# Mixer: the four z products of a block moved into the slot of ScalarE's silu pass, and silu of z read from PSUM

## The reference

```python
def mamba2_mixer(xn, in_proj_w, conv_w, conv_b, dt_bias, A_log, D_skip, rms_w, out_proj_w):
    zxbcdt = xn @ in_proj_w
    z = zxbcdt[..., :D_INNER]
    xBC = zxbcdt[..., D_INNER:D_INNER + CONV_DIM]
    dt = zxbcdt[..., D_INNER + CONV_DIM:]
    dt = jax.nn.softplus(dt + dt_bias)
    xBC = jax.nn.silu(causal_conv1d(xBC, conv_w, conv_b))
...
    y = ssd_scan(xh, dt, Bm, Cm, A)
    y = y + D_skip[None, None, :, None] * xh
    y = y.reshape(*y.shape[:-2], D_INNER)
    y = y * jax.nn.silu(z)
    y = y * jax.lax.rsqrt(jnp.mean(jnp.square(y), axis=-1, keepdims=True) + 1e-05) * rms_w
    return y @ out_proj_w
```

## Time and profile before

| | us |
|---|---|
| median of 3 runs | 3185.32 (3183.98 to 3193.42) |
| the profiled execution, its own time | 3180.88 |
| its span | 3179.2 |
| PE busy | 2799.2 (88%) |
| DVE busy | 1839.9 (58%) |
| ACT busy | 1384.6 (44%) |
| POOL busy | 678.1 (21%) |

### The profile page before, as it was taken

The page is one execution under the profiler, slowest core; times in us unless marked ns, Lnnn a source line. Parts: engine busy times, 40 slices in busy tenths (PEclk is TensorE's granted clock), DMA queues, the critical chain, the costliest instruction groups (busy, mean ns, idle before and its releaser), DMA issues. The chain is left out here.

```text
span 3179.2 us, 46142 instructions
## 1 busy us (share of the span) xinstructions
PE 2799.2 (88%) x16998; PEld 2086.3 (66%) x16998; DVE 1839.9 (58%) x3504; ACT 1384.6 (44%) x2394; POOL 678.1 (21%) x716
## 2 busy tenths in 40 slices
PE   0488888888888888869999799999999999999999
PEld 0354555455555555458888687887878787878787
DVE  4688888888888888746767433333333333333332
ACT  0566666666666666536555322222222222222221
POOL 5022222222222222210000122222222222222221
PEclk6799989998999899879999899999999999999999
DMA  3010101010101010035211100000000000000000
GB/s 125 29 35 20 35 20 35 20 35 20 35 21 35 21 35 11 28 104 208 70 62 64 48 13 7 11 14 16 14 16 14 16 14 16 14 16 14 16 14 8
DMA packets 104858, 107.06 MB, mean 34 GB/s; under 512 B 35897, under 2 KB 98617, under 8 KB 102977
## 3 DMA queue, kind: packets, MB, share of 16 engines
q1 hardware_dynamic: 99520, 103.81, 10.1%
q10 hardware_dynamic: 5120, 0.19, 0.1%
HBM read 71.41 MB, written 40.94 MB: 35 GB/s over the span
## 5 line engine op out<-in xcount | busy, mean ns | idle before, releaser
L1597 PE MATMUL fbank<-hid,fw 128*128 128x512 f32 x4096 | 962.3, 395 | 0.0
L1597 PEld LDWEIGHTS fbank<-hid,fw 128*128 128x128 f32 x4096 | 766.1, 187 | 187.0
L1747 DVE TENSOR_TENSOR hid<-fhf,hid 128x512 fp32r<-128x512 f32 x384 | 264.9, 690 | 704.3 <-POOL hid L1704 704.3
L1704 POOL TENSOR_SCALAR hid<-fhf 128x512 fp32r<-128x512 f32 x384 | 271.1, 706 | 1040.2 <-ACT fhf L1676 760.8
L808 ACT ACTIVATE mh<-ebank 128x512 f32<-128x512 f32 x512 | 302.0, 598 | 415.0 <-PE ebank L663 413.8
L1121 DVE SCALAR_TENSOR_TENSOR mh<-mh,gm 128x512 f32<-128x512 f32 x512 | 403.2, 794 | 1.8 <-ACT mh L808 1.8
L663 PE MATMUL ebank<-cright,cleft 102*128 102x512 bf16 x512 | 211.1, 413 | 64.1 <-ACT cin L847 28.9
L1676 ACT ACTIVATE fhf<-fbank,sh2c 128x512 f32<-128x512 f32 x128 | 88.0, 688 | 382.4 <-PE fbank L1597 382.4
L676 PE MATMUL yin<-mh,xpad 128*32 128x128 f32 x4096 | 230.5, 300 | 27.1 <-DVE mh L1121 26.6
L650 PE MATMUL ebank<-ah,win 128*128 128x512 f32 x640 | 246.7, 425 | 7.1 <-ACT cin L847 6.6
L1676 ACT ACTIVATE fhf<-fbank,sh1c 128x512 f32<-128x512 f32 x128 | 88.1, 688 | 320.8 <-PE fbank L1597 320.6
(11 more groups left out here) (180 smaller groups left out, 4380.1 us busy)
## 6 DMA issues: line engine op xcount, KB each, us to landing
fx<-x_d SPq DMA_DIRECT2D x17, 512.0 KB, 3.9
xs<-in_x SPq DMA_DIRECT2D x16, 512.0 KB, 4.3
h_d<-in_h SPq DMA_DIRECT2D x16, 512.0 KB, 5.4
o_d<-o SPq DMA_DIRECT2D x16, 512.0 KB, 2.9
mo<-o_d SPq DMA_DIRECT2D x16, 512.0 KB, 3.8
mx<-in_x SPq DMA_DIRECT2D x16, 512.0 KB, 4.8
x_d<-mx SPq DMA_DIRECT2D x16, 512.0 KB, 2.8
fw<-h_d SPq DMA_DIRECT2D x2, 4096.0 KB, 15.2
```

The source lines that it names most:

```text
L1597: mm = pe.matmul(bank[banks.slot(key)][:], w[:, k, m * P:(m + 1) * P].bitcast(dt), h[:, k, :].bitcast(dt), start=(k + n == 0), stop=(k == ...
L1704: pool.tensor_scalar(hid[i % 2][0][:, m, :], hf[j % 3][:], 1.0, 0.0, ALU.mult, ALU.add)\
L1747: dve.tensor_tensor(hid[i % 2][1][:, m, :], hf[j % 3][:], hid[i % 2][0][:, m, :].bitcast(F32), ALU.subtract).then_inc(c_lo.sem, 1)
```

## The change

The tables `Z_AT` and `Z_EVAC_AT` go. All four z products of a block stand on PE at the end of slot 26, one behind the other, and in the ring of `ebank` in the same place. `keep_z` goes. `gates` first runs the silu pass over xc, once the conv is done, and then four silus that read z's banks in PSUM and write sz. POOL's first multiplication of a block waits for the release of the last z bank rather than for the pass over xc.

```diff
-Z_AT = (17, 19, 21, 23)
-Z_EVAC_AT = (18, 20, 22, 24)
...
-            if n in Z_AT:
-                yield ("in", j, Z_AT.index(n))
+            if n == SILU_AT:
+                for m in range(QI):
+                    yield ("in", j, m)
...
-                    if n in Z_AT:
-                        in_proj(j, Z_AT.index(n))
+                    if n == SILU_AT:
+                        for m in range(QI):
+                            in_proj(j, m)
...
-            def keep_z(j, m):
-                key = ("in", j, m)
-                made(act, key)
-                if m == 0 and j >= 2:
-                    act.wait_ge(c_yg.sem, c_yg.at(0, NC * (j - 1)))
-                nc.scalar.activation(sz[j % 2][:, m, :], tile(key)[:], ACT.Copy).then_inc(free(key), 1)
-
             def gates(j):
-                released(act, ("in", j, QI - 1))
-                nc.scalar.activation(sz[j % 2][:], sz[j % 2][:], ACT.Silu)
                 act.wait_ge(c_conv.sem, c_conv.at(0, XM * (j + 1)))
                 nc.scalar.activation(xc[j % 2][:], xc[j % 2][:], ACT.Silu).then_inc(c_xc.sem, 1)
+                if j >= 2:
+                    act.wait_ge(c_yg.sem, c_yg.at(0, NC * (j - 1)))
+                for m in range(QI):
+                    key = ("in", j, m)
+                    made(act, key)
+                    nc.scalar.activation(sz[j % 2][:, m, :], tile(key)[:], ACT.Silu).then_inc(free(key), 1)
...
-                    if n in Z_EVAC_AT:
-                        keep_z(j, Z_EVAC_AT.index(n))
...
                 if q % NC == 0:
-                    pool.wait_ge(c_xc.sem, c_xc.at(0, q // NC + 1))
+                    released(pool, ("in", q // NC, QI - 1))
```

## The result

The changed kernel took 3274.66 us (median of 4 runs, 3271.05 to 3275.54), the kernel before 3185.69 us in the same comparison. The ratio is 1.027, 95% interval 1.0252 to 1.0287: 89 us slower. The forecast was 3248 us, the range 3199 to 3290.

What follows compares the result with a forecast made beforehand. It took DVE's variance of slot 17, through POOL, slot 24's projection and ACT's dx, as the bound. Terms 0.85 + 3.2 + 0 = 4.05 us times 15 blocks, plus 1.5, gave 62 us: 3248 us, range 3199 to 3290.

Steps and rivals of the forecast that it cites:

- What bounds the kernel: In the mixer, DVE waits for ACT's dx in slot 26; the path leads back through POOL to DVE's variance of slot 17.
- PE's 6.0 us of relief: The four z products leave slots 17, 19, 21, 23, relieving PE of 6.0 us per block; gain costed at nothing.
- Rival B: PE was the bound of slots 17 to 24: up to 5.1 us per block come free, 3110 us; chance 5%.
- The order in the hole: During ACT's silu pass in slot 26, z products and their silus end dx at 753.9 instead of 753.06: plus 0.85 us per block.
- The clock ahead of the slot: With z gone from slots 18 to 24, PE's clock falls to 1.2 GHz at slot 24's projection: plus 3.2 us per block.
- The rule of the Trainium skill: Clock lost only to one long idle gap between matmul bursts; so full through slots 18 to 24, that term nothing.
- Rival A: The clock is kept, slot 24's projection at 2.4 GHz: minus 10 us in all, 3175 us; chance 9%.
- The clock behind the hole: PE's clock at slot 32's projection, after z in slot 26: between minus 1.6 and plus 2.4 us per block, taken as 0.
- The first block: Same ACT order with nothing beside it, one product more behind the xc pass: plus 1.5 us once.
- Rival C: The clock is low through slot 26's z products too, or their banks wait on ACT: 9.7 us per block, 3332; chance 4%.
- the z products have the full clock: The z products in slot 26, starting 8 to 9 us after slot 24's projection, run at full clock, 1.49 us each.

Runs made afterwards that it cites:

- The first fill experiment: Changed kernel plus idle PE matmuls, 4 before each decay of slots 18 to 24 and 6 before slot 24's projection: 3221.63 us, ratio 1.0102 to the kernel before.

## Why the prediction was right or wrong

**What bounds the kernel: right.** In all 14 blocks in question DVE's variance of slot 17, POOL and the projection of slot 24 stand in a row, and the projection starts 5.05 to 5.08 us behind the variance in both kernels. The projection waits for POOL, 2.33 us now in place of 1.18, and PE's 6.0 us of relief gave nothing. Rival B is out.

**The order in the hole: right, 1.0 us for 0.85.** From the silu table load to the end of dx it was 8.92 us (744.14 to 753.06, rows 8) and is 9.96 us (788.26 to 798.22). The silu of z from PSUM took 0.60 us alone, as taken, and three in a row took 1.56; the fourth waited 0.77 us for its product.

**The clock ahead of the slot: right, 3.3 us for 3.2.** The projection of slot 24 takes 3.72 to 3.79 us in every one of these blocks. From the variance to the table load it was 11.1 us everywhere; it is 12.8 to 13.2 us in 6 of the 14 and 15.3 in 8, on average 14.4. In the block shown: 772.96 to 788.26, 15.3. The first fill experiment takes this back in full. The rule of the Trainium skill that was weighed ("TensorE: Matmul & The Clock Gate", "HAM oscillation — how this bites in real kernels") did not hold here: no long idle gap went ahead of the fall. The window 770 to 774 is at 0.53 already, and the gaps on PE just ahead were 1.26 and 0.77 us (the first two rows of PE above), with one group of masked products between them; the 2.33 us ahead of the projection came later. In 13 of the 14 blocks no gap on PE in the 5 us ahead of this fall had lasted longer than 1.3 us when the clock fell; in the second block one was 2.6 us. Rival A is out.

**The clock behind the hole: mis-sized, 2.1 us where I took 0.** This is the step that made the forecast 27 us too low. The text named both ends, minus 1.6 and plus 2.4, and the mechanism at the upper end is what came: PE runs out of work behind z, the clock falls before the projection of slot 32 (3.78 us in all blocks, in place of 3.1 to 3.8), and returns later, so that the sums behind it take 1.71 us too. From the addends of slot 25 to those of slot 33 it was 17.0 us on average of 14 blocks and is 19.1; the windows above show 0.50 still in 802 to 806. From there to the next variance 0.6 us came back, which nothing in my sum had; its cause stays open. The terms are 1.0 + 3.3 + 2.1 - 0.6 = 5.8 us, against 6.0 between the second and the fifteenth xc pass, and 5.5 with the first and the last interval. The first block cost 0.85 us, where I took 1.5: its variance of slot 17 came at 184.76 us in place of 183.91.

**Rival C: out.** In all 15 blocks that have four z products in slot 26 the granted clock is 1.0 through them, and they take 6.3 to 6.6 us together. In the block shown they stand behind 10 us of unbroken work on PE. The clock was back 0.8 us before they began, so "the z products have the full clock" was right with little to spare.

**Missed:** a second gate of DVE's addends, the masked product of slot 28, now behind the z products. It lies 2.5 us below dx, so it cost nothing in the change as made, but it bounds what a cure of dx can give.

## What to carry to other kernels

Work that is off the path can still pay: if it is what holds TensorE's clock in front of a step that is on the path, moving it away slows that step. Here five of six matmuls of the z products were taken out of the kernel before, and it went from 3185 to 3217 us. So before moving matmuls out of a stretch, ask which matmuls behind them are waited for, and price those at 1.2 GHz. When a hole is to be filled, ask which engine pays for it. Here it was DVE, waiting for one ACT result that could be made before the hole; moving just that, and leaving the z products where they were, gained 0.6%, and 1.2% with idle matmuls in the hole. Look at every place that such a move touches: the same move in all chunks cost 0.8%.

## What was not expected of the hardware

Taking five of six matmuls of z away made the kernel before 31 us slower, and adding 42 idle ones per block to the changed kernel made it 96 us faster. The sums of squares behind the projection, one column wide, also slow down at the low clock, from 0.95 to 1.71 us (781.60 above). In the kernel before:

```profile
739.96 0.95 PE L698 MATMUL bank<-ones,ysq 128*128 128x1 f32 x8
```

And the clock came back late: in the block shown PE was busy from 778.02 on, and the granted clock was still 0.50 in 782 to 786.
